# A decoder layer in fp32: the last batch's projection and routing in one program with the experts

## The reference

```python
x = _layernorm(x + attn(x, Wq, Wk, Wv, Wp, bp))
x = _layernorm(x + xattn(ctx_1024, x, conv_w, conv_b, 512, 512, 4))
expert_inputs = jnp.einsum('bnd,bnec->becd', x, dispatch)   # dispatch: at most 128 tokens per batch and expert
h = jax.nn.gelu(jnp.einsum('becd,edh->bech', expert_inputs, W1))      # 256 -> 1024
expert_outputs = jnp.einsum('bech,ehd->becd', h, W2)                  # 1024 -> 256
output = jnp.einsum('becd,bnec->bnd', expert_outputs, combine)
x = _layernorm(x + output)
```

## Time and profile before

| | us |
|---|---|
| three timed runs | 2065.3, 2067.49, 2070.75 |
| their median | 2067.49 |
| the profiled execution | 2063.77 |
| its span in the trace | 2062.0 |

### The profile page before, as it was taken

The page is one execution under the profiler, slowest core; times in us unless marked ns, Lnnn a source line. Parts: engine busy times, 40 slices in busy tenths (PEclk is TensorE's granted clock), DMA queues, the critical chain, the costliest instruction groups (busy, mean ns, idle before and its releaser), DMA issues. The chain is left out here.

```text
span 2062.0 us, 30533 instructions
## 1 busy us (share of the span) xinstructions
PE 1927.1 (93%) x11352; PEld 1274.6 (62%) x11352; DVE 1356.0 (66%) x2252; ACT 875.9 (42%) x1092; POOL 1362.4 (66%) x717
## 2 busy tenths in 40 slices
PE   7999999999999999899999999999999986669996
PEld 5565666566666666556666565566666643558886
DVE  5566666667676666767666658676666676446775
ACT  3444444444444454344435443343454532324542
POOL 1787777778656776686758666886567766125554
PEclk8999999999999999999999999999999997759998
DMA  4200000012111100122102000211111002322330
GB/s 145 78 21 17 22 17 21 21 56 77 49 31 46 33 21 16 32 78 80 45 11 62 16 21 17 83 37 42 37 41 39 25 11 82 118 93 93 126 127 34
DMA packets 150076, 104.22 MB, mean 51 GB/s; under 512 B 74028, under 2 KB 136620, under 8 KB 148908
## 3 DMA queue, kind: packets, MB, share of 16 engines
q1 hardware_dynamic: 146860, 93.82, 15.2%
q0 software_dynamic: 3072, 8.46, 1.2%
HBM read 69.15 MB, written 29.43 MB: 48 GB/s over the span
## 5 line engine op out<-in xcount | busy, mean ns | idle before, releaser
L920 POOL TENSOR_TENSOR prob_sum<-prob_sum,probs 128x1024 f32<-128x1024 f32 x384 | 924.3, 2407 | 230.0 <-ACT probs L1129 188.6
L1193 DVE TENSOR_REDUCE max_of<-spare_ps 128x1 f32<-128x512 f32 x1024 | 656.2, 682 | 355.6 <-PE spare_ps L1012 344.3
L1129 ACT ACTIVATE probs<-score_ps 128x1024 f32<-128x1024 f32 x512 | 516.1, 1027 | 540.3 <-PE score_ps L1033 530.7
L1047 PE MATMUL av_ps<-probs,v 128*64 128x512 f32 x2048 | 468.6, 600 | 5.0 <-issue 4.5
L1012 PE MATMUL spare_ps<-k_hi,q_hi 64*128 64x512 f32 x1024 | 293.8, 560 | 32.1 <-DVE max_of L1193 23.8
L1012 PEld LDWEIGHTS spare_ps<-k_hi,q_hi 64*128 64x128 f32 x1024 | 167.0, 306 | 230.2 <-issue 216.5
L1047 PEld LDWEIGHTS av_ps<-probs,v 128*64 128x64 f32 x2048 | 139.6, 137 | 271.2 <-issue 255.5
L916 POOL TENSOR_TENSOR prob_sum<-probs 128x1024 f32<-128x1024 f32 x64 | 153.2, 2394 | 194.2 <-ACT probs L1129 194.2
L1204 DVE RECIPROCAL sums<-sums 128x128 f32<-128x128 f32 x256 | 233.5, 932 | 28.4 <-ACT sums L1141 28.4
L1033 PE MATMUL score_ps<-q_hi,k_hi 64*128 64x512 f32 x1024 | 215.4, 401 | 1.3 <-DVE o_in L1217 0.9
L1033 PE MATMUL score_ps<-shift_rows,one_rows 64*128 64x512 f32 x1024 | 212.3, 395 | 0.0
(11 more groups left out here) (184 smaller groups left out, 2356.3 us busy)
## 6 DMA issues: line engine op xcount, KB each, us to landing
o_transposed<-o_out SPq DMA_DIRECT2D x64, 256.0 KB, 2.0
w_raw<-in_L_ffn_W_dram SPq DMA_DIRECT2D x16, 1024.0 KB, 5.8
o_in<-o_transposed SPq DMA_DIRECT2D x26, 512.0 KB, 4.0
w_raw<-in_L_attn_Wq_dram SPq DMA_DIRECT2D x64, 64.0 KB
w_raw<-in_L_attn_Wk_dram SPq DMA_DIRECT2D x64, 64.0 KB
wv_raw<-in_L_attn_Wv_dram SPq DMA_DIRECT2D x32, 128.0 KB
x<-in_x_dram SPq DMA_DIRECT2D x4, 1024.0 KB, 5.6
xT_kept<-x_transposed SPq DMA_DIRECT2D x4, 1024.0 KB, 6.7
```

The costliest lines, as they stand in the source:

```text
L920: pool.tensor_tensor(out, out, probs[:, n % RING], ALU.add).then_inc(prob_added, 1)
L1047: last = pe.matmul(av_ps[hd * E:(hd + 1) * E, :], v[:, quad % 2, kt, 2 * first_head + hd, :], probs[:, n % RING, hd, :], start=(kt == 0), ...
L1129: act.activation(probs[:, n % RING], score_ps[n % 2][:, :, :], ACT.Exp).then_inc(probs_ready, 1)
L1193: dve.tensor_reduce(max_of[:, u % 2, kh, j, hd:hd + 1], bank[:, :], AX.X, ALU.max).then_inc(pass_read, 1)
```

## The change

- The second and the third program become one, `build_tail`, without a barrier between them. The order on every engine is written out by hand.
- Experts 0 and 1 are done for the tiles of the first three batches (passes 0 and 1) between the steps of the last batch's chain. After the routing come passes 2 and 3, each the one tile of the last batch for expert 0 and 1, and then passes 4 to 9, experts 2 to 7 with four tiles.
- Weights have two split buffers, by the parity of the expert; the second lies in the space of the split Wp and of two of the three buffers for the split attention output. There is still one raw buffer for W1 and one for W2. W1 of expert p is split after the up product of pass p, W2 of expert p-1 behind the first four gelus of pass p; since pass p is expert p-2, that is one expert earlier than before.
- On SP the rows `xe` of expert e are loaded between its W1 and its W2.
- The last batch's first two tiles are loaded at the end of the attention program. Half of each of the two norms moves from ACT to DVE (`norm_last`); `move` waits for both halves. The projections share two PSUM banks; the gates' scores are read by one copy.

```diff
-        sp.wait_ge(self.x1_done, TB * (b + 1))
+        sp.wait_ge(self.x1_done, TB * (b + 1) if b < self.B - 1 else TB * b + HT)
...
+    def norm_last(self, dve, i, rows, done):
+        for t, row in rows:
+            dve.tensor_scalar(row, row, self.moments[i][:, t, 0:1], self.scale[i][:, t:t + 1], ALU.subtract, ALU.mult
+                              ).then_inc(done, 1)
...
+            sp.wait_ge(o_stored[0], 16 * UNITS // 2)
+            for t in range(2):
+                route.load_o(sp, TILES * (B - 1) + t)
...
+        self.high = [[self.flat(first_high[i]), second_high[i]] for i in range(2)]
+        self.low = [[self.flat(first_low[i]), second_low[i]] for i in range(2)]
...
     def load(self, sp, i, e):
+        if e > 0:
+            self.wait_split(sp, i, e - 1)
...
+    EARLY = 2
+    PASSES = [(e, 0, B - 1) for e in range(EARLY)] + [(e, B - 1, RT) for e in range(EARLY)]
+    PASSES += [(e, 0, RT) for e in range(EARLY, EX)]
+    LATE = EARLY
...
+        second = [[wp[:, :, :].rearrange(flat), split[:, 0:2].rearrange("p a b c -> p (a b c)")]
+                  for wp, split in ((route.wp_hi, route.splits[0]), (route.wp_lo, route.splits[1]))]
...
+        proj_bank = [y_bank[2 + t % 2] for t in range(TB)]
+        x2T_bank = [h_ps[g % 2] for g in range(TB // 2)]
+        late_bank = y_bank[B - 1]
...
-            sp.wait_ge(route.sent, 16 * TB * EARLY_BATCHES)
-            load_xe(0, (0, EARLY_BATCHES), xe_first_in)
-            sp.wait_ge(late_sent, 16 * TB * (B - EARLY_BATCHES))
-            load_xe(0, (EARLY_BATCHES, RT), xe_in[0])
-            load_xe(1, (0, RT), xe_in[1])
-            for e in range(1, EX):
-                weights.wait_split(sp, 0, e - 1)
...
+            for t in range(2, TB):
+                route.load_o(sp, T0 + t)
+                if t in (3, 5):
+                    weights.load(sp, (t - 3) // 2, 0)
+            sp.wait_ge(route.sent, 16 * TB * (B - 1))
+            load_xe(0, 0, B - 1, xe_early_in[0])
+            route.load_new(sp, b)
+            route.load_cw(sp, b)
+            load_xe(1, 0, B - 1, xe_early_in[1])
+            weights.load(sp, 0, 1)
+            weights.load(sp, 1, 1)
+            sp.wait_ge(route.x1_low_done, HT)
+            route.move(sp, b)
+            weights.load(sp, 0, 2)
+            weights.load(sp, 1, 2)
+            sp.wait_ge(late_sent, 16 * TB)
+            for e in range(EARLY):
+                load_xe(e, B - 1, RT, xe_in[e])
+            load_xe(EARLY, 0, RT, xe_in[EARLY])
+            for e in range(EARLY + 1, EX):
                 weights.load(sp, 0, e)
-                weights.wait_split(sp, 1, e - 1)
+                load_xe(e, 0, RT, xe_in[e % XE_RING])
                 weights.load(sp, 1, e)
-                if e + 1 < EX:
-                    load_xe(e + 1, (0, RT), xe_in[(e + 1) % XE_RING])
...
+            route.number_tokens(pool, b)
+            weights.split_low(pool, 0, 0)
+            weights.split_low(pool, 1, 0)
+            for t in (2, 0):
+                route.add_moved(pool, b, t, route.sum_done)
+            weights.split_low(pool, 0, 1)
+            weights.split_low(pool, 1, 1)
             for i in range(2):
-                route.send(pool, B - 1, i, late_sent)
-            for e in range(EX):
-                if e > 0:
-                    split_w2(e)
-                if e + 1 < EX:
-                    split_w1(e + 1)
-                if e > 0:
-                    send(e - 1)
-            send(EX - 1)
+                route.send(pool, b, i, late_sent)
+            send(0)
+            for p in range(LATE, len(PASSES)):
+                if LATE < p <= EX:
+                    weights.split_low(pool, 1, p - 1)
+                if p < EX:
+                    weights.split_low(pool, 0, p)
+                send(p - 1)
+            send(len(PASSES) - 1)
...
+            for t in range(TB):
+                if t > 1:
+                    pe.wait_ge(route.z_done, T0 + t - 1)
+                route.project(pe, T0 + t, proj_bank[t])
+            transpose_rows(0)
+            up(0, range(6))
+            pe.wait_ge(route.z_done, T0 + TB)
+            route.transpose_old(pe, b, late_bank)
+            up(0, range(6, HC))
+            route.compress(pe, b, late_bank)
+            down(0)
+            transpose_rows(1)
+            for g in range(TB // 2):
+                if g < 2:
+                    pe.wait_ge(gelu_done, HC)
+                else:
+                    pe.wait_ge(route.x2T_done, TB // 2 * b + g - 1)
+                route.transpose_x2(pe, b, g, x2T_bank[g])
+            pe.wait_ge(route.x2T_done, TB // 2 * (b + 1))
+            up(1, range(2))
+            for g in range(TB // 2):
+                pe.wait_ge(route.comp_added, b + 1)
+                route.score_experts(pe, b, g, late_bank[:, 2 * EX * g:2 * EX * (g + 1)])
+            up(1, range(2, 5))
+            route.count(pe, b, late_bank)
+            up(1, range(5, HC))
+            down(1)
+            transpose_rows(LATE)
+            pe.wait_ge(route.counts_out, b + 1)
+            for p in range(LATE, len(PASSES)):
+                up(p, range(HC))
+                if p + 1 < len(PASSES):
+                    transpose_rows(p + 1)
+                down(p)
...
+            for t in range(TB):
+                route.split_high(act, T0 + t)
+                if t >= TB - 2:
+                    for j in range(weights.PIECES):
+                        weights.split_high(act, t - TB + 2, 0, j)
             rows_high(0)
...
+            route.take_root(act, 0, b)
+            for c in range(2):
+                gelu(0, c)
+            route.norm1(act, b, range(HT, TB))
+            for c in range(2, HC):
+                gelu(0, c)
+            split_w1(1)
+            route.take_root(act, 1, b)
+            route.norm2(act, b, range(HT))
+            for g in range(TB // 2):
+                route.x2T_out(act, b, g, x2T_bank[g])
+            rows_high(1)
+            for c in range(2):
+                gelu(1, c)
+            route.exp_gates(act, b)
+            for c in range(2, HC):
+                gelu(1, c)
+                if c < 2 + weights.PIECES:
+                    split_w2(1, c - 2)
+            take_root(0)
+            rows_high(LATE)
+            for p in range(LATE, len(PASSES)):
                 for c in range(HC):
...
+                    gelu(p, c)
+                    if LATE < p <= EX and c < weights.PIECES:
+                        split_w2(p - 1, c)
                 if p + 1 < len(PASSES):
                     rows_high(p + 1)
...
+                if p < EX:
+                    split_w1(p)
+                take_root(p - 1)
+            take_root(len(PASSES) - 1)
...
+            route.find_scale(dve, 0, b)
+            route.norm_last(dve, 0, [(t, route.x1[:, t, :]) for t in range(HT)], route.x1_low_done)
+            for c in range(2):
+                split_h(0, c)
+            route.place_old(dve, b, late_bank)
+            for c in range(2, 6):
+                split_h(0, c)
+            for t in (4, 6):
+                route.add_moved(dve, b, t, half_sum_done)
+            route.rows_stats(dve, b, range(HT, TB), half_sum_done, -2)
+            for c in range(6, HC):
+                split_h(0, c)
+            route.add_compressed(dve, b, late_bank)
+            route.rows_stats(dve, b, range(HT), route.sum_done, route.PLACES * b)
+            route.aggregate(dve, 1, b)
+            route.find_scale(dve, 1, b)
+            route.norm_last(dve, 1, [(t, route.x2[:, t, 0:D]) for t in range(HT, TB)], route.x2_high_done)
+            rows_low(1)
+            add_rows(0)
+            for c in range(2):
+                split_h(1, c)
+            route.read_all_logits(dve, b, late_bank)
+            route.choose(dve, b)
+            split_h(1, 2)
+            route.find_mask(dve, b)
+            split_h(1, 3)
+            route.tally(dve, b)
+            split_h(1, 4)
+            route.read_counts(dve, b, late_bank)
+            route.find_free(dve, b)
+            split_h(1, 5)
+            route.find_rows(dve, b)
+            for c in range(6, HC):
+                split_h(1, c)
+            norm(0)
+            add_rows(1)
+            rows_low(LATE)
+            for p in range(LATE, len(PASSES)):
                 for c in range(HC):
...
+                    split_h(p, c)
                 if p + 1 < len(PASSES):
                     rows_low(p + 1)
...
+                norm(p - 1)
+                add_rows(p)
+            norm(len(PASSES) - 1)
```

335 lines of the change are left out of this document (130 added, 205 removed).

## The result

The changed kernel takes **2092.61 us** (median of 4 runs, 2089.43 to 2093.09) against 2067.8 for the kernel before on the same chip: a ratio of 1.0116, 95% interval 1.0099 to 1.0134. It is slower, as forecast (2093, 2074 to 2108). Its profiled execution took 2092.3, with a span of 2090.6 and a mean granted clock of 0.965 (before: 2063.77, 2062.0 and 0.969). The two profiled executions differ by 28.5 us, the two medians by only 24.8.

A forecast was written before the change was run, and what follows sets the result against it. PE was taken to bound the experts' passes (busy 23.9 of 25.6 us), a dependency chain the stretch ahead. Terms -7 + 34.8 - 1.7 + 3 = +29 on the profiled 2063.8 gave 2093 us, range 2074 to 2108.

The forecast's parts named there:

- (a) The early loads: Last batch's projections: tiles loaded before save 4.2 us, less 1.0 for DVE splits; end about 1771.8 instead of 1775.0.
- (b) The chain: From projections to row numbers: early expert work delays the steps; row numbers about 1842, 14.5 us later than before.
- (c) The narrow passes: Row numbers to expert 2: first narrow up product about 1857.5; expert 2 starts at 1888 or 1889, 7 us earlier.
- The later passes: Experts 2 to 7: W2 behind xe makes ACT wait before the second gelu; +34.8 us in all.
- The clock: Up products after stalls: 1.2 GHz may return; 0.7 us charged for each of four passes, 3 in all.
- the clock stays down: Rival, chance 0.12: each stalled pass loses 4 us instead of 0.7, and pass 4 too; 2107.
- The last pass: Last expert pass: no split runs beside it any more, so its 1.7 us of lost time go.
- weights in time: Rival, chance 0.10: W2 lands before ACT reaches its first piece, ACT never waits; 2055.
- Cheap interleaving: Rival, chance 0.14: DVE's extra chunks fit chain waits, narrow passes at full clock; expert 2 18 to 20 us earlier, 2081.

The follow-up runs named there:

- e4: Changed kernel with W1 and W2 of expert 0 loaded behind all six attention output tiles instead of between them; 2090.65 us, a single run.
- e11: The changed kernel itself measured once more, nothing edited; ratio 1.0134 against the kernel before.
- e7: On top of e1, the chain's steps go ahead of early expert work on PE, DVE and ACT; ratio 0.9954 against the kernel before.
- e1: Changed kernel with W2 again loaded ahead of the rows xe on SP, nothing else; 2059.45 us, ratio 0.9970 against the kernel before.
- e2: Changed kernel with ACT's four W2 pieces behind gelus 4 to 7 instead of 0 to 3; 2075.0 us, ratio 1.0039 against the kernel before.
- e3: Kernel before with only SP's order changed, xe loaded ahead of W2; 2099.1 us, ratio 1.0158.
- e10: Changed kernel with W2's split moved beside the down product and the stores ahead of it; ratio 0.9968 against the kernel before.
- e9: e10 with the chain-first order of e7 added; 2046.3 us, ratio 0.9921 against the kernel before.
- e6: On top of e1, POOL sends expert 1's three stores behind the split of expert 2's W2; 2065.38 us, ratio 0.9985 against the kernel before.
- e8: On top of e1, the next W2's split moved beside the down product, behind W1's split; 2058.11 us, ratio 0.9956 against the kernel before.
- e5: On top of e1, unread matmuls keep PE busy around the first narrow pass's transposes; ratio 0.9980 against the kernel before.

## Why the prediction was right, and where it was right by luck

**(a) The early loads.** PE's first projection starts 2.4 us after the block instead of 6.7: the 4.2 are there. The projections then end 27.8 after the start instead of 31.0, a gain of 3.2; I had 3.2 (4.2 less 1.0). The reason I gave for the 1.0 (DVE beside POOL) is not what the trace shows: PE is busy 24.9 us instead of 24.4, and stands for 0.4, which e4 takes away.

**(b) The chain.** From the projections' end to the issue of the move 7.5 (7.8 taken), to the sum 11.5 (11.4), to the second norm 13.8 (13.9), from the norm to the scores' end 15.1 (16), to the row numbers 19.2 (21). The rows that show the steps, of ACT and DVE in the changed kernel, and of DVE's two chunks that stand in it (first those, with the row numbers below them, then the norm; before: the earlier trace rows):

```profile
1796.41 1.32 DVE L1698 CAST h_hi<-h_act 128x384 fp32r<-128x384 f32 x1
1799.18 1.42 DVE L1698 CAST h_hi<-h_act 128x384 fp32r<-128x384 f32 x1
1840.91 0.17 DVE L599 CAST send_to<-row 128x8 uint32<-128x8 f32 x1
```
```profile
1806.63 2.08 ACT L317 ACTIVATE x<-x,shift,scale 128x256 f32<-128x256 f32 x4 [0.47 <-DVE shift L474]
```

The row numbers come 94.8 after the block's start; I had 98 (1842 less 1743.98). In e11, the same program, they come at 98.6. The argument, that what stands ahead of the chain's steps on an in-order list is paid, holds, and e7 shows that the reverse gives 9.4 us back at the issue of the load.

**(c) The narrow passes** took 10.3, 5.3, 12.3 and 5.8 us against 9.5, 5, 11 and 6. Between the row numbers and the first narrow up product I took 15.5, and the trace has 19.0: 4.9 of them from the first transposes to the up product, where e1 and e2 have 1.4. The term that was too small is this one, "with 2 us to land and 2 us to transpose and split": the landing took 2.1, the other 4.9. The four parts of the narrow passes add 2.2 more, and against these two stand the row numbers, 3 us early. Hence expert 2 at 147.4 from the block's start, not 144 to 145, and a gain of 3.4 (in the profile of e11 none) instead of **7**.

**The later passes.** W2 issued 0.41 behind xe: exact. Landing 6.4 us after issue (6.7). ACT's waits are 9.6, 3.1, 6.5, 7.0 and 6.4, in all 32.6, against 10, 3.3 and three times 7.2, in all 34.8. This term carried the forecast, and e1, e2 and e3 show its two parts, the order on SP and the place on ACT's list.

**The clock.** The first matmul pair behind the stall took 1.22 us instead of 0.63, and the granted clock over such a pass is 0.89, against 1.00 before. Yet the passes grew by 32.1 where the waits sum to 32.6, and against e1 each of passes 5 to 8 grew by 0.4 to 0.5 less than its own wait. The slow chunks were hidden under DVE's splits: PE's later wait for these splits, 1.46 us in the kernel before, is 0.79, nothing and 0.48 in passes 6 to 8. The 3 us charged were not paid. The rival "the clock stays down" fell with them, and its 2107. The Trainium skill (TensorE: Matmul & The Clock Gate, What's actually happening) says that the default state is throttled and that activity releases it; the trace agrees, with a granted clock of 0.78 while PE all but stood (1961 to 1966) and 0.64 in the 5 us behind (1967 to 1972), but here it cost nothing.

**The last pass** took 2.2 less (1.7).

The sum was +29, with -7, +34.8, -1.7 and +3. The profile has -1.3 (-3.4, and 2.1 of chance ahead of the block), +32.1, -2.2 and nothing. So in the passes 5.7 us too much were charged (37.8 with the clock's 3, against 32.1), and ahead of them 5.7 too little, of which 2.1 is that chance; the two errors cancelled. There is a second piece of luck. The sum stood on a profiled execution that lay 3.7 below its median, and by it the median could as well have been 2097; I gave 2093. The changed kernel's profiled execution lies 0.3 below its own median, so the medians differ by 24.8 and not by 29. What the rival "weights in time" supposed, at a price of 2055, was made true by e1's edit (2059.45): the gain of the rest of the change is real but small, 0.3%, once the order is right. "Cheap interleaving" (18 to 20 us earlier) did not come with the change; with the edits of e7 and e10 together e9 gets 16.4.

## What to carry to other kernels

When a load is moved on a queue, look up what the load now ahead of it waits for, and then where its first consumer stands on its own in-order list. The price is not the transfer's delay as such but that everything behind the consumer waits with it: here 32.6 us of waits made the passes 32.1 us longer. A split or copy that is not needed in this stage should not stand in front of work that is, and an engine that shares its ports with another should be given it where that other has no deadline. Work put into a chain's holes delays the chain if it stands ahead of the chain's steps on an in-order list: this chain was stretched by 15 us, and moving such work behind its steps brought 9.4 back.

## What the runs showed that I had not expected

- One DVE operation of 0.23 us stood for 5.62 us beside four uninterrupted POOL pieces of 1.23 us; in e6, with a break after two of them, the longest took 1.26.
- The scores (32 small matmuls) take 3.9 to 4.2 us in four profiles (changed, e1, e2, e8) and 6.8 in five (e4, e5, e6, e10, e11), as in the kernel before; the program up to there is the same but for e4. They are where xe is issued at 106 to 107 or at 111. PE has gaps in that stretch, and its clock differs from run to run: 0.50 around the scores of e11 (1817.0 to 1825.3), 0.89 around those of the changed kernel's first profile (1815 to 1822). About 1 us of the later issue is there before the scores, at the issue of the move (36.3 against 35.2).
- From the first narrow transposes to the up product it is 1.4 to 1.7 us in e1, e2 and e4, 2.3 to 2.4 in e7 and e9, and 4.5 to 5.2 in the six others. In the changed kernel DVE and ACT are released together, at 1857.00 and 1857.14, 1.6 us after the recorded end of the transposes, by an event that the profile does not name. The row is

```profile
1857.00 1.27 DVE L1709 SCALAR_TENSOR_TENSOR y<-y_ps,xe 128x256 f32<-128x256 f32 x3 [12.93 <-remote]
```

  What it is stays open; no run here was made to find it. The two effects are each about 3 us. Expert 2's start of one and the same program varies between 147.4 and 151.0, by the scores and what lies ahead of them, since both of its profiles have the long lag. Differences of that size between single profiles (e5, e6 and e10 against e1) were not read as effects of an edit.
